# A Mamba block followed by a routed mixture of experts: the lower parts of the gate and up weights made after the scan

## The reference, cut to what matters

```python
# x (4,256,256), ctx (4,256,128)
def reference(...):
    # 1: a Mamba block over ctx, gated by layernorm(x)
    xi = in_proj(ctx); u = silu(causal_conv4(xi) + conv_b)
    dt_lo, Bm, Cm = split(x_proj(u))                 # 8, 16, 16
    delta = softplus(dt_proj(dt_lo) + dt_proj_b)
    # for each of 16 states n, along 256 time steps:
    #   s[t] = s[t-1] * exp(delta[t] * A[n]) + delta[t] * u[t] * B[n, t]
    #   y[t] += s[t] * C[n, t]
    x = x + tanh(g_xattn) * ((y + D * u) * silu(layernorm(x)))
    # 2: a routed mixture, 8 experts, the best 2 for each token
    t = layernorm(x); w, idx = softmax(top2(t @ gate_w))
    for e in range(8):
        h = silu(t @ w0[e]) * (t @ w1[e])            # 256 -> 512
        out += cw[:, e] * (h @ wo[e])                # 512 -> 256
    return x + tanh(g_ffn) * out
```

## Time and profile before

| | us |
|---|---|
| median of 3 runs (340.27 to 341.49) | 341.0 |
| the profiled execution | 341.57 |
| its span, first to last instruction | 339.8 |
| mean granted clock of TensorE, of full speed | 0.885 |
| start of the first scan step's scan, and of the last's | 39.55, 180.4 |
| `gated(1, 1)` starts | 187.12 |
| the first expert product starts | 212.54 |

### The profile page before, as it was taken

The page is one execution under the profiler, slowest core; times in us unless marked ns, Lnnn a source line. Parts: engine busy times, 40 slices in busy tenths (PEclk is TensorE's granted clock), DMA queues, the critical chain, the costliest instruction groups (busy, mean ns, idle before and its releaser), DMA issues.

```text
span 339.8 us, 4549 instructions
## 1 busy us (share of the span) xinstructions
PE 265.8 (78%) x1093; PEld 174.1 (51%) x1094; DVE 246.7 (73%) x450; ACT 176.8 (52%) x327; POOL 185.0 (54%) x162
## 2 busy tenths in 40 slices
PE   3976687747898857574866957999999999999960
PEld 4522142313444414232321645798899889988950
DVE  3757999999999896989995886356655655565540
ACT  2495386545476549344667061245655565566540
POOL 4001348995799759293999403234465446545331
PEclk9987558997999789696999775799999999999996
DMA  6799000000000000300007731112332333233221
GB/s 192 241 379 379 7 1 0 2 1 0 0 1 0 2 1 0 123 1 0 0 2 237 254 126 32 39 22 50 64 48 48 60 62 46 46 62 62 30 23 25
DMA packets 18910, 22.69 MB, mean 67 GB/s; under 512 B 2624, under 2 KB 14062, under 8 KB 18894
## 3 DMA queue, kind: packets, MB, share of 16 engines
q1 hardware_dynamic: 13312, 16.39, 13.9%
q0 software_dynamic: 4416, 6.03, 11.0%
q10 hardware_dynamic: 1166, 0.08, 0.2%
HBM read 17.38 MB, written 5.11 MB: 66 GB/s over the span
## 4 chain that ended last, share of the span: by engine, by line
PE 48%; DVE 20%; issue 13%; POOL 8%; ACT 5%; DMA 2%; POOLq 1%; SPq 0%; DVEq 0%; ACTq 0%
PE PD L865 10%; PE PZ L901 10%; PE PU L865 10%; PE PY L733 7%; POOL hC L390 7%; DVE states L1036 5%; DVE states L1042 4%; PE PY L887 3%; DMA xs<-in_x 2%; PE PY L695 2%; PE PZ L858 2%; PE PU L725 2%; POOL W_lo L381 1%; PE PY L847 1%; PE PU L842 1%
## 5 line engine op out<-in xcount | busy, mean ns | idle before, releaser
L390 POOL TENSOR_TENSOR hC<-states,WO 128x512 f32<-128x512 f32 x64 | 82.6, 1304 | 35.7 <-PE PY L733 20.4
L733 PE MATMUL PY<-hC,ident 128*128 128x512 f32 x128 | 78.9, 702 | 12.8 <-POOL hC L390 12.4
L1042 DVE TENSOR_TENSOR_SCAN states<-PD,states 128x512 f32<-128x512 f32 x64 | 77.5, 1212 | 0.2 <-ACT PD L541 0.2
L425 POOL DMA_INDIRECT out<-lg,y_at x23 | 36.4, 1585 | 55.8 <-ACT lg L627 52.2
L541 ACT ACTIVATE PD<-WO,Aneg 128x510 f32<-128x510 f32 x64 | 44.0, 688 | 40.0 <-DVE states L1042 35.8
L1309 DVE TENSOR_TENSOR WO_lo<-WO,WO_hi 128x512 fp32r<-128x512 f32 x46 | 29.8, 689 | 34.5 <-ACT WO_hi L620 33.9
L620 ACT ACTIVATE WO_hi<-WO 128x512 fp32r x46 | 26.5, 624 | 47.0 <-PE PZ L901 46.8
L1036 DVE TENSOR_TENSOR states<-PU,WO 128x512 f32<-128x512 f32 x64 | 43.0, 673 | 2.5 <-POOL hC L390 2.4
L725 PE MATMUL PU<-BC,sel 128*128 128x512 f32 x32 | 20.5, 640 | 28.7 <-DVE states L1036 28.7
L733 PEld LDWEIGHTS PY<-hC,ident 128*128 128x128 f32 x128 | 26.3, 224 | 29.8 <-POOL hC L390 24.5
L412 POOL DMA_INDIRECT hC<-x_rows,x_at x23 | 23.3, 1014 | 29.1 <-DVE x_at L1265 15.0
(11 more groups left out here) (221 smaller groups left out, 498.6 us busy)
## 6 DMA issues: line engine op xcount, KB each, us to landing
W<-in_L_ffn_w SPq DMA_DIRECT2D x16, 512.0 KB, 11.0
WO<-in_L_ffn_wo SPq DMA_DIRECT2D x8, 512.0 KB, 4.5
xs<-in_x SPq DMA_DIRECT2D x1, 1024.0 KB, 7.9
x_rows<-u SPq DMA_DIRECT2D x2, 512.0 KB, 2.8
out<-xs SPq DMA_DIRECT2D x2, 512.0 KB, 3.8
early<-in_ctx SPq DMA_DIRECT2D x1, 512.0 KB, 4.2
hC<-x_rows,x_at POOLq DMA_INDIRECT x23, 2.8
out<-lg,y_at POOLq DMA_INDIRECT x23, 3.8
```

The source lines that it names most:

```text
L390: pool.tensor_tensor(hC[:, n % 2, :], states[:, n % RING, :], C_rep[:, pair % C_RING, :], ALU.mult).then_inc(hc_done, 1)
L425: pool.indirect_dma_start(out=out, out_offset=bass.IndirectOffsetOnAxis(ap=y_at[:, s:s + 1], axis=0), in_=y_tile[s % 2], in_offset=None, c ...
L733: pe.matmul(PY[:, h, :], ident[:, :], hC[:, n % 2, :], start=(m == 0), stop=(m == DS - 1)).then_inc(y_done, 1)
L1042: dve.tensor_tensor_scan(states[:, n % RING, :], DEC[n % 2], states[:, n % RING, :], 0.0, ALU.mult, ALU.add).then_inc(scan_done, 1)
```

## The change

All 28 subtractions of GpSimd and the four of VectorE stay the same operations on the same blocks; they change place and engine. GpSimd makes none inside the scan any more, and the first ten behind its last product. VectorE makes 22: two behind `gated(1, 1)`, four behind `rows_hot(0)`, four behind `rows_hot(1)`, and twelve where it made four. ScalarE's upper parts stay where they were. The waits of TensorE follow from the same constant (10 and 22).

```diff
@@
-POOL_SPLITS = 28
+POOL_SPLITS = 10
+DVE_SPLITS = (POOL_SPLITS, 12, 16, 20, len(SPLITS))
@@
                     pool.tensor_tensor(hC[:, n % 2, :], states[:, n % RING, :], C_rep[:, pair % C_RING, :], ALU.mult).then_inc(hc_done, 1)
-                    if n in SPLIT_AT:
-                        lower(SPLIT_AT.index(n))
@@
-            for i in range(len(SPLIT_AT), POOL_SPLITS):
+            for i in range(POOL_SPLITS):
                 lower(i)
@@
+            def lower(at, end):
+                for i in range(at, end):
+                    dve.wait_ge(W_hi_ok, i + 1)
+                    dve.tensor_tensor(lo_part(i), whole_part(i), hi_part(i), ALU.subtract).then_inc(W_lo_dve, 1)
@@
             gated(1, 0, 2)
             gated(1, 1, 3)
+            lower(DVE_SPLITS[0], DVE_SPLITS[1])
             best_two(1)
             residual(1, 0)
             residual(1, 1)
             variance(1)
             rows_hot(dve, 0)
+            lower(DVE_SPLITS[1], DVE_SPLITS[2])
             places(1)
             rows_hot(dve, 1)
+            lower(DVE_SPLITS[2], DVE_SPLITS[3])
@@
-            for i in range(POOL_SPLITS, len(SPLITS)):
-                dve.wait_ge(W_hi_ok, i + 1)
-                dve.tensor_tensor(lo_part(i), whole_part(i), hi_part(i), ALU.subtract).then_inc(W_lo_dve, 1)
-
+            lower(DVE_SPLITS[3], DVE_SPLITS[4])
```

## The result

| | before | after |
|---|---|---|
| median, us | 341.23 (340.27 to 341.49, 4 runs) | 346.92 (346.58 to 347.49, 4 runs) |
| after / before | | 1.0189 [1.0153, 1.0224] |
| profiled execution, us | 341.57 | 346.58 |
| its span, us | 339.8 | 343.8 |
| mean granted TensorE clock | 0.885 | 0.864 |

The change costs 5.7 us by the medians. The profiled spans are 4.0 us apart.

The account below looks back on a forecast made before the run. VectorE was taken to bound most of the scan and the bridge, GpSimd the scan's stretches with subtractions. Scan and tail -8.5 plus bridge +13.1 gave +4.6 us on 341.0: 345.6 us, range 339.2 to 349.

Parts of the forecast that it names:

- (a): Scan: VectorE's eight waits for GpSimd's products all go, giving back 3.3 us.
- (b): Scan: VectorE operations held while GpSimd works get shorter, 2.1 us for a pair and 0.7 for the one at 57.91.
- (c): Scan, `places(0)`: VectorE waits for TensorE's ranks anyway, which swallows 0.2 us of the gain.
- (d): Tail, last scan to `gated(1, 1)`: with GpSimd caught up it takes 4.1 instead of 6.7 us, gain 2.6.
- (e): Bridge, `gated(1, 1)` to `residual`: lower parts, cast, `hot` and `mask` take turns with GpSimd's ten, +6.1 us.
- (f): Bridge: four subtractions on VectorE behind `rows_hot(0)`, with no wait to hide them, +2.5 us.
- (g): Bridge: four subtractions behind `rows_hot(1)`, 2.5 us less the 1.19 us table wait, +1.3 us.
- (h): Bridge: twelve subtractions instead of four behind `slot_w` delay the first gate product, +3.2 us.
- (i): Gate: TensorE starts at its lower clock level again, counted 0, bounds 0 and +1.7 us.
- the second rival: Bridge: no lock between GpSimd and VectorE, so faster, 339.2 us; chance 0.2 together with a scan that gains more.
- The first: Bridge: locks cost little, VectorE's small operations go through together, sum +0.4, 341.4 us; chance 0.15.
- The third: Scan: it gives little back, gain near 4 us, sum +9, 350 us; chance 0.1.

Follow-up runs that it names:

- without the 28: The kernel before with all 28 of GpSimd's subtractions left out, VectorE keeping its four: 331.14 us, ratio 0.9769 to the kernel before.
- with two subtractions out: The kernel before with only GpSimd's subtractions at scan steps 46 and 48 left out: 337.96 us, ratio 0.9876 to the kernel before.
- The second profile of after: The changed kernel timed again on a second chip, no edit: 345.24 us, ratio 1.0117 to the kernel before.
- the ten held back: The changed kernel with GpSimd's ten subtractions held until the second half's mask is made: 346.45 us, ratio 1.0191 to the kernel before.
- the memset kernel: The changed kernel with GpSimd's ten subtractions made into memsets of the same blocks: 339.77 us, ratio 0.9975 to the kernel before.

## Why the prediction was right, point by point

**What bounds the kernel.** As read. In the scan GpSimd's round of two products and a subtraction was the bound in stretches, and VectorE is it without; in the bridge VectorE was and is.

**(a) the waits, 3.3.** In after the steps 20, 22, 24, 48, 54 and 56 to 62 lost 1.51 + 0.67 + 1.08 = 3.3 us, and no wait of a drive for GpSimd is listed. Counting 0.1 us for each wait on top of the listed 2.4 was needed. The drives of steps 48 and 54 still came 0.17 and 0.18 us late in the first profile, and not in the second, where TensorE was at its upper level in step 37.

**(b) the held operations, 2.1 + 0.7.** The pair gave 1.6 in after, 2.07 without the 28 and 1.95 with two subtractions out; the operation at 57.91 gave 0.6. The 0.5 by which after falls short lies mostly in VectorE's wait for TensorE's ranks, 1.5 us in after and 1.1 without the 28: the term (c), counted at 0.2. The second profile of after had 1.1 us there and the full 2.07, so this too goes with the run.

**The scan's sum, 5.9.** 5.2 measured in the first profile, 6.1 without the 28, 7.4 and 5.2 in the other two profiles of after. The terms that belong to the change sum to 5.4, and the rest goes with TensorE's level in step 37 and its neighbours, for which the forecast had no term of its own in the scan. "About 135 instead of 140.9" was 135.7.

**(d) the tail, 2.6.** 2.4. The gate came 4.30 us after the last scan, where I reckoned 4.1: `gated(1, 0)` took 1.59, counted at 1.4. `gated(1, 1)` stands at 179.87 where I gave 178.6: the scan began 0.3 later and gave back 0.7 less, and the tail 0.2 less.

**(e), 6.1.** 5.7 measured, the largest term. Each lower part 1.48 ("1.2 or more"), each `hot` 1.21, `mask` 1.19. The cast was held, 0.92 against 0.17, which no row of before showed; without it the term would have been 4.9. The Trainium skill, "SBUF — State Buffer", section "Who interferes with whom", names casts among the operations that can take the ports GpSimd needs; by that rule the trace agrees. One turn of GpSimd for each such operation was the right count for this order of operations; all turns together came out 0.4 shorter. It isn't a rule: with the ten held back, `row_hot` and `blocksum` cost VectorE nothing.

**(f), (g), (h): 2.5, 1.3, 3.2.** 2.4, 1.1 and 2.8. The table's wait of 1.19 is gone, as said. (h) was mis-sized by 0.4: the twelve took 7.31 instead of 7.47, and `xT_lo` ends 0.64 us behind them, where I counted 0.85 for `w_at` and `split_x(0)`. Of (f) and (g) a wait was neither added nor left over; these two are read from the stages, and no kernel without them was tried.

**(i) the clock, 0.** The gate starts with the same two products in 1.22 us as in the earlier trace rows, and the loop is 0.8 us shorter, not longer. In the twelve other profiles it took 125.2 to 127.5.

**The sum.** +4.6 forecast, +4.0 by the spans, +5.7 by the first medians, +4.1 and +2.9 by the medians on the two other chips. The sum is nearer than its parts, which is luck: the bridge grew by 12.0 where 13.1 was forecast, scan and tail gave 7.6 where 8.5 was, and the stages where nothing was forecast moved by +0.3 and -0.8. Two bounds of the forecast are off by 0.2: by its own terms scan and tail give at most 8.9, not 9.1, and the second rival's better end is -1.8, which is what its 339.2 goes by, not -2.0.

**The rivals.** The first (small operations go through together) is excluded by the rows at 185.67 to 190.20. The second (no lock) is what the memset kernel makes real: 339.77, where I gave 339.2. The third (the scan gives little) needed a gain near 4; scan and tail gave 7.6 in the first profile and up to 9.8.

## What to carry to other kernels

Work moved into an engine's waits costs nothing only while it fits them: here 18 more subtractions of 0.62 us, 11.2 in all, met 5.3 us of idle time. Ask of a second engine's work what it reads and what runs beside it: ten GpSimd subtractions beside five VectorE operations that read SBUF twice and a cast cost 5.6 us, the same number of memsets nothing, and two plus three subtractions at places where VectorE reads PSUM or gathers statistics 0.3 us. In the router the count of such VectorE operations set the price, not their size, since GpSimd's next operation was running each time; a chain of small ones was the worst neighbour, and one of 1024 columns that began just ahead of GpSimd's paid nothing.

## What the runs showed of the hardware

A VectorE operation of 32 columns beside GpSimd's subtractions took 1.2 us, about as long as one of theirs; with nothing beside it, it took 0.18 or 0.19. GpSimd's loss is smaller: its ten took 13.20 us beside the router and 15.13 beside `row_hot` and the four lower parts, that is 1.32 and 1.51 us each, where four alone took 4.94, 1.24 each. A TENSOR_SCALAR with one SBUF operand of 4 columns took 0.49 instead of 0.17 at the same place where GpSimd subtracts, while the statistics, MAX8 and FIND_INDEX8 kept their lengths.

An indirect gather that GpSimd issues beside VectorE's twelve subtractions took 3.60 us on its engine, 213.64 to 217.24, where it took 0.95 in before and with four subtractions. It was so in each of the six profiles with the twelve, 3.59 to 3.61, and in none of the eight with four. Nothing in the bridge waited for it. Whether the subtractions held it was not tried by itself.

The same kernel's scan took 133.5 to 135.7 us in three profiles with a mean granted clock of 0.882, 0.864 and 0.868. The stretch ahead of the first scan, the same code in all fourteen profiles, took 37.8 to 40.1 us. A difference of 2 us in these stages on one profile is no evidence; the bridge of after, where VectorE is the bound, repeated to 0.03 us.
